# Graph convolution in three layers: more source tiles as float32r halves, count blocks loaded in fifths, and a two-input instruction on VectorE to widen the counts

## The chip, the cores and the metric

One core of a Trainium2 chip. The time is that of the device for one execution, in microseconds (us). TensorE is called PE here, VectorE DVE, ScalarE ACT, GpSimd POOL and SyncE SP, as the profile names them.

## The reference, cut to what matters

```
N, E, D, ED = 12500, 212500, 64, 16      # nodes, edges sorted by dst, row and edge widths
def conv(h, W, b):
    m = concatenate([h[dst], h[src], edge_attr], axis=1) @ W + b
    return segment_sum(m, dst, num_segments=12500)
h = relu(conv(x, W1, b1))
h = relu(conv(h, W2, b2))
out = layernorm(x + conv(h, W3, b3))
```

All in float32, with 12,500 loops (each node to itself) among the 212,500 edges.

## The kernel before, in words

Since the product is linear, the kernel sums the source rows of each target first and multiplies by `W` afterwards. The sum over edges is itself a product: a matrix of edge counts (source node by target node) times the rows. The nodes stand in 100 tiles of 125 (`TILES`), and 25 batches of 4 tiles or 500 nodes (`BATCHES`, `T`, `B`). A **batch** `g` is one group of 500 targets in one layer; `g` runs from 0 to 74, layer 0 is 0 to 24, layer 1 is 25 to 49, layer 2 is 50 to 74 (`LAST` is 50).

The first 375 targets of a batch (`DENSE`) go through the counts: for each of the 100 source tiles, a block of 125 by 375 counts in fp8. The other 125 targets (`FAR`) go edge by edge: POOL gathers their source rows with 18 indirect DMAs of 128 rows (`gather_rows`, L788), DVE makes 18 masks in one instruction (`make_far_masks`, L1182, 2250 elements a partition), and PE adds 36 small products (`sum_far`, L1519 and L1523).

Layer 0 builds the counts and stores them in HBM, then applies them. Layers 1 and 2 only load and apply them. In the program a batch of these layers is this on PE:

- Each row in float32 is kept as three bf16 parts. A source tile costs two matmuls of 375 columns: the **wide** one takes parts 0 and 1 side by side (128 columns of weights, `apply_wide`, L1461), the **narrow** one part 2 (64 columns, `apply_narrow`, L1490).
- In layer 2, 60 of the 100 tiles (the batches in `SPLIT`, 15 **units** of 4 tiles) are instead kept as two float32r halves side by side, and cost one matmul of 376 columns (`apply_split`, L1477). Its moving operand must be float32r too, so the fp8 counts of the unit's 4 tiles are first widened into a ring of 3 buffers (`spread`, `SPREAD_RING`): even units by ACT (`spread_act`, L917), odd units by DVE (`spread_dve`, L1371). A spread of unit `u` waits on `spread_used` until PE has used unit `u` - 3.
- Units and wide tiles alternate; the narrow matmuls come at the end of each of four quarters (`QUARTERS`).
- Between the quarters stand the steps of the batch before: `turn_h` (transposes) after the first, half of `conv` (the product with `W`) after the second, its other half after the third. At the end of the batch stands `sum_far`.
- After `conv`, DVE does `make_nodes` (L1255 on: in layer 1 the relu and the split into parts and halves, in layer 2 the residual and layernorm). Each engine runs its own list in order, so a spread behind `make_nodes` waits with it.

SP loads the counts in halves of 50 tiles (`load_block`), into three slots (`SLOTS`). POOL may be up to two batches ahead: `gather_rows` of batch `g` waits on `far_summed` for batch `g` - 2, and at the start of a layer for the rows of the whole layer before. The masks have two buffers and the same wait.

```
nc.vector.tensor_copy(spread[0:L, u % SPREAD_RING, :, 0:DENSE], counted(g, t, T)).then_inc(dve_spread, 1)
nc.tensor.matmul(acc_ps(g, slice(0, WIDE)), halves[0:L, i, j, :, :].rearrange("p k d -> p (k d)"),
                 spread[0:L, u % SPREAD_RING, j, :], start=(i == 0 and j == 0), stop=False)
```

Of the kernel before, what the change touches and what calls it, by code (L numbers as in the profile page):

```python
# [5 lines left out]
def gnn_kernel(nc, x, src, dst, edge_attr, weights, out):  # L6
# [18 lines left out]
    N, D = x.shape  # L25
# [30 lines left out]
    QUARTERS = [0, 24, 50, 74, TILES]  # L56
    HALF = TILES // 2
    SLOTS = 3
    WIDE = DENSE + 1
    SPREAD_RING = 3  # L60
    WHOLE = [0, 1, 4, 8, 10, 12, 15, 18, 19, 22]
    SPLIT = [b for b in range(BATCHES) if b not in WHOLE]
    UNITS_OF = [[b for b in SPLIT if QUARTERS[q] <= b * T < QUARTERS[q + 1]] for q in range(4)]
    TILES_OF = [[t for t in range(QUARTERS[q], QUARTERS[q + 1]) if t // T in WHOLE] for q in range(4)]
    assert all(b * T + T <= QUARTERS[q + 1] for q in range(4) for b in UNITS_OF[q])
# [47 lines left out]
    with ctx:  # L113
# [3 lines left out]
        def sem(name):  # L117
# [11 lines left out]
        HALVES = len(SPLIT) * T * 2 * D * 4  # L129
        halves_at = parts_at + len(SPLIT) * T * PARTS * D * 2 - HALVES  # L130
        assert halves_at % 32 == 0 and halves_at >= early_at + 4 * 768
        halves = nc.alloc_sbuf_tensor_at("halves", [P, len(SPLIT), T, 2, D], fp32r, offset=halves_at)
        staged = attr_stage[:, :, :].rearrange("p s c -> p (s c)")[:, 0:T * PARTS * D].bitcast(bf16).rearrange(
            "p (k t a d) -> p k t a d", k=2, t=T, a=PARTS)

        def whole_tile(layer, t):

            return WHOLE.index(t // T) * T + len(SPLIT) * T + t % T if layer == LAYERS - 1 else t

        blocks_at = -(-nc.sbuf_base // 32) * 32  # L140
# [63 lines left out]

        x_rows = is_key_flat[0:L, 0:4 * T * D].bitcast(fp32).rearrange(
# [101 lines left out]
        spread_used = sem("spread_used")  # L307
        spread_cleared = sem("spread_cleared")
# [20 lines left out]
        ALL = LAYERS * BATCHES  # L329
        LAST = (LAYERS - 1) * BATCHES  # L330
# [252 lines left out]
        def store_parts(engine, g):  # L583
# [36 lines left out]
        def wait_half(engine, g, t):  # L620

            n = half_of(g, t)
            engine.wait_ge(block_loaded[n % SLOTS], (n // SLOTS + 1) * DMA)

# [3 lines left out]
        def _(sp):  # L628
# [16 lines left out]
            def load_block(g, half):  # L645

                b = g % BATCHES
                n = 2 * (g - BATCHES) + half
                words = slice(half * HALF * DENSE // 2, (half + 1) * HALF * DENSE // 2)
# [64 lines left out]
            for g in range(BATCHES):  # L714
                for k in range(PER_BATCH):
# [9 lines left out]
                    if k == PER_BATCH - RING and g == BATCHES - 1:  # L725
                        for half in range(2):
                            load_block(BATCHES, half)
# [5 lines left out]
            for g in range(BATCHES + 1, ALL):  # L733
                for half in range(2):
                    load_block(g, half)
# [8 lines left out]
        def _(pool):  # L744
# [29 lines left out]
            def gather_rows(g, j):  # L774
                layer = g // BATCHES
                if j == 0:
                    if layer == 0:
                        pool.wait_ge(far_src_loaded[g % 2], (g // 2 + 1) * DMA)
                    if g % BATCHES <= 1:
                        stores = 1 if layer == 0 else BATCHES if layer < LAYERS - 1 else len(WHOLE)  # L780
                        pool.wait_ge(parts_stored[layer], stores * 2 * DMA)
                        if layer == LAYERS - 1:
                            pool.wait_ge(staged_stored[0], (len(SPLIT) + 1) // 2 * 2 * DMA)
# [893 lines left out]
```

## Time and profile before

| what | value |
| --- | --- |
| median of 3 runs | 2837.05 us (2836.85 to 2837.15) |
| the profiled execution: its own time | 2837.66 us |
| the profiled execution: its span, first to last instruction | 2835.8 us |
| PE busy | 2680.3 us, 95% of the span |
| DVE, ACT, POOL busy | 61%, 55%, 57% |
| mean granted clock of PE, as a share of full speed | 0.985 |
| moved by DMA | 498.04 MB |

Layer 0 fills the span up to 1396.7 us, layer 1 follows to about 2137 us, layer 2 to the end. The rows that the prediction reads stand further down. In a line of the timeline the columns are: start (us from the span's start), duration (us; of a run of equal instructions, the whole of it), engine, line, operation, what it writes and reads, and count; in brackets the idle time before it and what ended that. A matmul's recorded duration is longer than its share of the pipeline, so the cost of one is read from the distance between starts.

### The profile page before, as it was taken

What the parts mean: (1) busy time and instruction counts of PE and PEld (TensorE: products, weight loads), DVE (VectorE), ACT (ScalarE), POOL (GpSimd) and SP (SyncE); (2) the same over time, 40 slices, a digit from 0 to 9 for tenths busy, and PEclk for the clock granted to TensorE, in tenths of its full rate; (3) what the DMA queues carried; (4) which work ended last, traced back from release to release, by engine and by line L of the source; (5) the groups of instructions that cost most, each with busy time, mean ns of one, the idle gap of its engine ahead of it and who ended that gap; (6) DMA issues with size and microseconds to landing.
All of it is one profiled execution on the core that took longest, in us unless ns stands there. A gap on an engine that the chain in (4) does not pass through costs nothing.

```text
span 2835.8 us, 56920 instructions
## 1 busy us (share of the span) xinstructions
PE 2680.3 (95%) x21643; PEld 1690.4 (60%) x21643; DVE 1724.7 (61%) x4026; ACT 1567.2 (55%) x2535; POOL 1624.4 (57%) x1391
## 2 busy tenths in 40 slices
PE   1599999999999999999989999999998899999998
PEld 0155555555555555555656666666666666666666
DVE  7999999999999999999412111111113444444443
ACT  5699898998989989989200000000003444444444
POOL 5355344353453544535277666666644777777775
PEclk9699999999999999999999999999999999999999
DMA  4543434435344343353656666666655666666663
GB/s 94 132 137 112 176 110 144 143 110 179 108 130 159 109 168 119 113 176 110 228 195 221 207 215 214 223 218 218 220 204 185 217 227 226 241 232 223 237 239 108
DMA packets 224957, 498.04 MB, mean 176 GB/s; under 512 B 150353, under 2 KB 186183, under 8 KB 208688
## 3 DMA queue, kind: packets, MB, share of 16 engines
q1 hardware_dynamic: 120196, 277.89, 27.9%
q10 hardware_dynamic: 57404, 146.14, 13.8%
q0 software_dynamic: 47088, 70.34, 10.0%
q8 instruction: 179, 2.93, 0.4%
q14 instruction: 90, 0.74, 0.1%
HBM read 347.58 MB, written 146.61 MB: 174 GB/s over the span
## 4 chain that ended last, share of the span: by engine, by line
PE 86%; DVE 6%; POOL 3%; ACT 2%; issue 2%; DMA 1%; SPq 0%; ACTq 0%; POOLq 0%; DVEq 0%
PE ps L1461 32%; PE ps L1490 18%; PE ps L1431 14%; PE ps L1477 7%; PE ps L1558 3%; PE ps L1519 3%; PE ps L1509 3%; POOL far_rows L788 3%; PE ps L1559 2%; PE ps L1523 2%; PE ps L1544 1%; ACT spread L917 1%; PE ps L1533 1%; ACT blocks L850 1%; DVE is_key L1131 1%
## 5 line engine op out<-in xcount | busy, mean ns | idle before, releaser
L788 POOL DMA_INDIRECT far_rows<-parts,far_src x1350 | 1570.7, 1163 | 1157.1 <-DMA far_src<-in_src 570.3
L1461 PE MATMUL ps<-blocks,parts 125*128 125x375 fp8e4 x6000 | 1351.4, 325 | 4.1 <-ACT blocks L850 2.4
L850 ACT ACTIVATE blocks<-ps 128x505 fp8e4<-128x505 f32 x1875 | 1118.0, 759 | 129.3 <-PE ps L1431 126.5
L1461 PEld LDWEIGHTS ps<-blocks,parts 125*128 125x128 bf16 x6000 | 557.6, 99 | 406.4 <-issue 52.5
L1431 PE MATMUL ps<-is_key,is_low 128*128 128x505 bf16 x1875 | 701.6, 384 | 31.8 <-DMA w_own<-in_L_gnn_W 14.0
L1131 DVE TENSOR_SCALAR is_key<-from_one,parts 128x500 bf16<-128x500 f16 x1875 | 596.4, 351 | 2.0 <-PE ps L1431 1.2
L1490 PE MATMUL ps<-blocks,parts 125*64 125x375 fp8e4 x6000 | 565.8, 327 | 0.0
L1490 PEld LDWEIGHTS ps<-blocks,parts 125*64 125x64 bf16 x6000 | 309.0, 110 | 244.5 <-issue 154.0
L917 ACT CAST spread<-blocks 125x1500 fp32r<-125x1500 fp8e4 x200 | 285.9, 1442 | 266.4 <-PE ps L1477 165.6
L1477 PE MATMUL ps<-spread,halves 125*128 125x376 f32 x1500 | 365.5, 366 | 28.8 <-ACT spread L917 22.4
L1371 DVE CAST spread<-blocks 125x1500 fp32r<-125x1500 fp8e4 x175 | 167.1, 956 | 329.7 <-PE ps L1477 329.7
L1121 DVE TENSOR_TENSOR is_low<-from_one,parts 128x640 bf16<-128x640 f16 x375 | 308.2, 822 | 16.0 <-PE ps L1431 12.6
L1431 PEld LDWEIGHTS ps<-is_key,is_low 128*128 128x128 bf16 x1875 | 185.2, 100 | 216.1 <-DVE is_key L1131 31.0
L1255 DVE COPY z<-ps 125x256 f32<-125x256 f32 x51 | 21.7, 425 | 480.4 <-PE ps L1559 480.4
L1477 PEld LDWEIGHTS ps<-spread,halves 125*128 125x128 f32 x1500 | 255.4, 190 | 64.6 <-ACT spread L917 39.7
L1182 DVE SCALAR_TENSOR_TENSOR far_masks<-far_dst,from_one 128x750 fp8e4<-128x750 int32 (+1 forms) x125 | 195.0, 1560 | 156.9 <-PE ps L1523 156.9
L876 ACT ACTIVATE node_rows<-z,node_deg 125x64 f32<-125x64 f32 x200 | 54.0, 367 | 372.0 <-DVE z L1255 350.3
L923 ACT COPY acc_sb<-ps 128x500 f32<-128x500 f32 x50 | 28.9, 577 | 210.2 <-PE ps L1523 210.2
L928 ACT COPY own_sb<-ps 64x500 f32<-64x500 f32 x50 | 28.5, 570 | 192.9 <-PE ps L1544 192.9
L1166 DVE SCALAR_TENSOR_TENSOR masks<-dst_stage,from_one 128x825 bf16<-128x825 int32 x125 | 126.4, 1011 | 0.0
L1558 PE MATMUL ps<-w_src,acc_sb 128*125 128x64 f32 x600 | 124.0, 288 | 0.7 <-ACT own_sb L928 0.7
L1558 PEld LDWEIGHTS ps<-w_src,acc_sb 128*125 128x125 f32 x600 | 88.5, 186 | 47.4 <-issue 43.7
(136 smaller groups left out, 1447.7 us busy)
## 6 DMA issues: line engine op xcount, KB each, us to landing
blocks<-counts SPq DMA_DIRECT2D x100, 2343.8 KB
counts<-blocks ACTq DMA_DIRECT2D x25, 4687.5 KB, 14.6
far_rows<-parts,far_src POOLq DMA_INDIRECT x1350
attr_stage<-in_edge_attr SPq DMA_DIRECT2D x125, 88.0 KB
h_rows<-rows ACTq DMA_DIRECT2D x49, 128.0 KB
own_sb<-attr_sums ACTq DMA_DIRECT2D x49, 95.7 KB
parts<-parts SPq DMA_DIRECT2D x1, 4200.0 KB
parts<-parts SPq DMA_DIRECT2D x24, 168.0 KB
```

The costliest lines, as they stand in the source:

```text
L788: nc.gpsimd.indirect_dma_start(far_rows[:, g % 2, j, :], None, parts_d[layer], bass.IndirectOffsetOnAxis(ap=far_src[:, g % BATCHES, j:j + ...
L850: nc.scalar.activation(blocks[:, b % 2, :, n * W:(n + 1) * W], build[:, c % BUILD, 0:COLS].rearrange("p (t w) -> p t w", w=W), ACT.Copy, s ...
L917: nc.scalar.copy(spread[0:L, u % SPREAD_RING, :, 0:DENSE], counted(g, t, T)).then_inc(act_spread, 1)
L1121: nc.vector.tensor_tensor(is_low[:, m % 2, :, :], from_one[:, 0:P].rearrange("p (a l) -> p a l", a=1).to_broadcast([P, LOWS, P]), lows[:, ...
L1131: nc.vector.tensor_scalar(is_key[:, c % KEY_RING, 0:KEYS], from_one[:, :], keys[:, b, n:n + 1], None, ALU.is_equal).then_inc(keyed, 1)
L1182: nc.vector.scalar_tensor_tensor(out=far_masks[:, g % 2, js, :], in0=far_dst[:, b, js].rearrange("p (j a) -> p j a", a=1).to_broadcast(shape),
L1371: nc.vector.tensor_copy(spread[0:L, u % SPREAD_RING, :, 0:DENSE], counted(g, t, T)).then_inc(dve_spread, 1)
L1431: nc.tensor.matmul(build[:, c % BUILD, 0:COLS], is_low[:, c // LOWS % 2, c % LOWS, :], is_key[:, c % KEY_RING, 0:COLS], start=True, stop=T ...
L1461: nc.tensor.matmul(acc_ps(g), parts[0:L, layer % 2, whole_tile(layer, t), 0:2, :].rearrange("p k d -> p (k d)"), moving, start=(t == 0 and ...
L1477: last = nc.tensor.matmul(acc_ps(g, slice(0, WIDE)), halves[0:L, i, j, :, :].rearrange("p k d -> p (k d)"), spread[0:L, u % SPREAD_RING, j ...
L1490: last = nc.tensor.matmul(acc_ps(g)[side:side + D, :], parts[0:L, layer % 2, whole_tile(layer, t), 2, :], moving, start=False, stop=(t >= ...
L1558: nc.tensor.matmul(z_ps[:, t, :], acc_flat[:, at], w_src[layer][:, :], start=True, stop=False)
```

## The change: what it does

- Layer 1 from its second batch on keeps 60 tiles as halves (3 of every 5 batches, `SPLIT_OF`), layer 2 keeps 80 (4 of every 5): 15 and 20 units in a batch. The first batch of layer 1 still takes 100 whole tiles.
- A batch goes in **fifths** of 20 tiles: 3 or 4 units alternating with the wide tiles, then 8 or 4 narrow matmuls. The steps of the batch before stand after fifths 0, 1 and 2. SP loads fifths into 6 slots.
- During the first batch of layer 1, DVE adds the three bf16 parts of 60 tiles and splits the sums into halves (`halve`, 12 instructions of 256 elements a partition for each fifth, 60 in all), which lie where parts and blocks lay.
- DVE widens a unit with `scalar_tensor_tensor` (count times one, then the larger of that and count), both inputs being the same fp8 counts in SBUF.
- The order on ACT and DVE is written anew, with spreads around each of the other steps. The flags of an input that the kernel can't handle are looked at somewhat later.

```
-    QUARTERS = [0, 24, 50, 74, TILES]
-    HALF = TILES // 2
-    SLOTS = 3
+    FIFTHS = 5
+    FIFTH = TILES // FIFTHS
+    GROUP_OF = FIFTH // T
+    SLOTS = 6
...
+    SPLIT_OF = [0, 3, 4]
...
+        def units_of(g):
+
+            return SPLIT_OF[g // BATCHES] if BATCHES < g < ALL else 0
...
+                        spread_act(h, 5, 3 * m + 2)
+                    if g + 2 < ALL:
+                        load_attr(act, g + 2)
+                    spread_act(h, 3 * m + 2, 3 * m + 4)
+                    give_rows(g)
+                    spread_act(h, 3 * m + 4, FIFTHS * m)
+                    give_nodes(g)
+                spread_act(h + 1, 0, 3)
...
-                    nc.vector.tensor_copy(spread[0:L, u % SPREAD_RING, :, 0:DENSE], counted(g, t, T)).then_inc(dve_spread, 1)
+                    nc.vector.scalar_tensor_tensor(out=spread[0:L, u % SPREAD_RING, :, 0:DENSE], in0=counted(g, t, T), scalar=1.0,
+                                                   in1=counted(g, t, T), op0=ALU.mult, op1=ALU.max).then_inc(dve_spread, 1)
+
+            def halve(q):
+
+                dve.wait_ge(block_used, q + 1)
+                order = [2, 1, 0]
...
+                for r in order:
+                    step(nc.vector.tensor_tensor(sums[0:L, r, :, :], three[r][0], three[r][1], ALU.add))
...
+                nc.vector.engine_nop().then_inc(halved, 1)
...
+            for g in range(BATCHES, ALL):
+
+                h = g + 1
+                m = units_of(h)
...
+                nodes_at = 7 if h % BATCHES == 0 else 3 * m + 2
+                spread_dve(h, 3, 5)
                 if g + 2 < ALL:
                     make_far_masks(g + 2)
-                spread_dve(g + 1, [9, 11, 13] if g == LAST else [5, 7, 9, 11, 13])
...
+                spread_dve(h, 5, nodes_at)
                 make_nodes(g)
...
+                spread_dve(h, nodes_at, FIFTHS * m)
+                spread_dve(h + 1, 0, 2)
...
+                for q in range(FIFTHS):
+                    tiles = range((q * GROUP_OF + m) * T, (q + 1) * FIFTH)
+                    for i in range(m):
+                        apply_split(g, q * m + i)
+                        for t in tiles[i * len(tiles) // m:(i + 1) * len(tiles) // m]:
```

In `spread_dve(g, first, stop)` the odd units from `first` up to `stop` are meant.

**DVE in a batch of layer 2.** Before: 5 spreads (units 5 to 13), the nodes, 2 spreads (1 and 3 of the next batch), the mask, and again.

```order
L1371 CAST spread<-blocks 125x4x375 x5
L1255 COPY z<-ps 125x256
L1277 TENSOR_TENSOR z<-z,is_key 125x256
L1278 TENSOR_REDUCE mean<-z 125x4
L1279 SCALAR_TENSOR_TENSOR z<-mean,z 125x256
L1281 TENSOR_TENSOR left<-z 125x256
L1282 TENSOR_REDUCE var<-left 125x4
L1284 RECIPROCAL rstd<-std 125x4
L1286 TENSOR_TENSOR node_rows<-z,rstd 125x256
L1371 CAST spread<-blocks 125x4x375 x2
L1182 SCALAR_TENSOR_TENSOR far_masks<-far_dst,from_one 128x2250
```

In the changed kernel the same stretch, L1429 being the spread, L1311 the first line of the nodes and L1238 the mask:

```order
L1429 SCALAR_TENSOR_TENSOR spread<-blocks 125x4x375 x5
L1311 COPY z<-ps 125x256
L1333 TENSOR_TENSOR z<-z,is_key 125x256
L1334 TENSOR_REDUCE mean<-z 125x4
L1335 SCALAR_TENSOR_TENSOR z<-mean,z 125x256
L1337 TENSOR_TENSOR left<-z 125x256
L1338 TENSOR_REDUCE var<-left 125x4
L1340 RECIPROCAL rstd<-std 125x4
L1342 TENSOR_TENSOR node_rows<-z,rstd 125x256
L1429 SCALAR_TENSOR_TENSOR spread<-blocks 125x4x375 x5
L1238 SCALAR_TENSOR_TENSOR far_masks<-far_dst,from_one 128x2250
```

Behind the nodes now stand 5 spreads, of which 3 (units 15, 17 and 19) are of the batch that PE is working on, and 2 (units 1 and 3) of the next.

**PE in a batch of layer 2**, from the transposes after the first part of a batch to the first half of `conv` (L1558; L1642 after the change). Before:

```order
L1544 MATMUL ps<-ident,h_rows 64x125 x4
L1477 MATMUL ps<-spread,halves 128x376 x4
L1461 MATMUL ps<-blocks,parts 128x375 x2
L1477 MATMUL ps<-spread,halves 128x376 x4
L1461 MATMUL ps<-blocks,parts 128x375 x3
L1477 MATMUL ps<-spread,halves 128x376 x4
L1461 MATMUL ps<-blocks,parts 128x375 x2
L1477 MATMUL ps<-spread,halves 128x376 x4
L1461 MATMUL ps<-blocks,parts 128x375 x3
L1490 MATMUL ps<-blocks,parts 64x375 x10
L1558 MATMUL ps<-w_src,acc_sb 125x64
```

After the change:

```order
L1628 MATMUL ps<-ident,h_rows 64x125 x4
L1561 MATMUL ps<-spread,halves_last 128x376 x4
L1546 MATMUL ps<-blocks,parts 128x375
L1561 MATMUL ps<-spread,halves_last 128x376 x4
L1546 MATMUL ps<-blocks,parts 128x375
L1561 MATMUL ps<-spread,halves_last 128x376 x4
L1546 MATMUL ps<-blocks,parts 128x375
L1561 MATMUL ps<-spread,halves_last 128x376 x4
L1546 MATMUL ps<-blocks,parts 128x375
L1574 MATMUL ps<-blocks,parts 64x375 x4
L1642 MATMUL ps<-w_src,acc_sb 125x64
```

Between two units there is now one wide matmul in place of two or three, and 4 narrow ones close the fifth in place of 10.

## Rows read from the trace of the kernel before

**Rows 1.** Windows, one batch of each layer: length, busy (count) per engine, clock.

```profile
1613.68:1642.75 29.07, 29.07 (x260) 18.81 (x257) 5.06 (x8) 2.21 (x6) 19.17 (x18) 1.00 0.61 214
2479.34:2506.06 26.72, 25.81 (x198) 18.41 (x197) 12.15 (x18) 12.79 (x11) 21.23 (x19) 1.00 0.67 232
```

**Rows 2.** Timeline, PE, a quarter of a batch of layer 1 and `sum_far`.

```profile
1605.43 4.37 PE L1461 MATMUL ps<-blocks,parts 125*128 125x375 fp8e4 x26
1609.73 2.27 PE L1490 MATMUL ps<-blocks,parts 125*64 125x375 fp8e4 x26
1611.93 1.20 PE L1519 MATMUL ps<-far_masks,far_rows 128*128 128x125 fp8e4 x18
...
1613.68 4.05 PE L1461 MATMUL ps<-blocks,parts 125*128 125x375 fp8e4 x24
```

**Rows 3.** Timeline, PE, units in layer 2.

```profile
2491.55 0.98 PE L1477 MATMUL ps<-spread,halves 125*128 125x376 f32 x4
...
2492.57 0.98 PE L1477 MATMUL ps<-spread,halves 125*128 125x376 f32 x4
...
2493.83 0.83 PE L1490 MATMUL ps<-blocks,parts 125*64 125x375 fp8e4 x8
...
2495.48 0.94 PE L1477 MATMUL ps<-spread,halves 125*128 125x376 f32 x4
```

**Rows 4.** Waits in a stretch of layer 1 (1500 to 2000 us), POOL's own.

```profile
POOL far_rows L788 <- PE ps L1523: 73.1, 16, 4.7
```

**Rows 5.** Waits in a stretch of layer 2 (2200 to 2700 us), POOL's only entry.

```profile
POOL far_rows L788 <- issue: 103.1, 338, 0.3
```

**Rows 6.** Durations (ns, min/median/max) of the mask and of the spread on DVE.

```profile
L1182 DVE SCALAR_TENSOR_TENSOR far_masks<-far_dst,from_one x125: 924/936/2505, 136.3 to 2773.4; 128x750 fp8e4<-128x750 int32 x75, 128x2250 fp8e4<-128x2250 int32 x50
...
L1371 DVE CAST spread<-blocks x175: 933/943/1192, 2131.5 to 2814.4; 125x1500 fp32r<-125x1500 fp8e4 x175
```

**Rows 7.** Timeline, DVE and POOL, a mask in layer 1.

```profile
1425.94 0.94 POOL L788 DMA_INDIRECT far_rows<-parts,far_src  x1 [0.30 <-issue]
...
1426.43 2.48 DVE L1182 SCALAR_TENSOR_TENSOR far_masks<-far_dst,from_one 128x2250 fp8e4<-128x2250 int32 x1
1427.18 2.55 POOL L788 DMA_INDIRECT far_rows<-parts,far_src  x1 [0.30 <-issue]
```

**Rows 8.** Timeline, POOL, layer 2; 18 gathers from 2506.57 to 2533.32.

```profile
2506.57 2.96 POOL L788 DMA_INDIRECT far_rows<-parts,far_src  x1 [0.30 <-issue]
...
2512.33 1.40 POOL L788 DMA_INDIRECT far_rows<-parts,far_src  x1 [0.30 <-issue]
2514.03 1.14 POOL L788 DMA_INDIRECT far_rows<-parts,far_src  x1 [0.30 <-issue]
...
2533.32 2.96 POOL L788 DMA_INDIRECT far_rows<-parts,far_src  x1 [0.30 <-issue]
```

**Rows 9.** Timeline, DVE, layer 2: the nodes and two spreads.

```profile
2495.71 0.42 DVE L1255 COPY z<-ps 125x256 f32<-125x256 f32 x1 [1.09 <-PE ps L1559]
...
2499.00 0.43 DVE L1286 TENSOR_TENSOR node_rows<-z,rstd 125x256 f32<-125x256 f32 x1
...
2511.97 0.94 DVE L1371 CAST spread<-blocks 125x1500 fp32r<-125x1500 fp8e4 x1 [2.56 <-PE ps L1477]
2514.11 0.94 DVE L1371 CAST spread<-blocks 125x1500 fp32r<-125x1500 fp8e4 x1 [1.20 <-PE ps L1477]
```

**Rows 10.** Timeline, DVE, the nodes of one batch of layer 1.

```profile
2070.78 0.42 DVE L1255 COPY z<-ps 125x256 f32<-125x256 f32 x1 [18.41 <-PE ps L1559]
...
2073.08 0.43 DVE L1273 TENSOR_TENSOR attr_stage<-left,attr_stage 125x256 bf16<-125x256 f32 x1
```

**Rows 11.** Waits of PE from 1390 us on: for the gathered rows.

```profile
PE ps L1519 <- DMA far_rows<-parts,far_src: 18.1, 2, 9.3
```

**Rows 12.** Windows: 8 us of PE from 2150 us, after it had stood still for 3.60 us.

```profile
2150.00:2158.00 8.00, 6.80 (x20) 4.76 (x21) 2.19 (x3) 3.38 (x3) 4.25 (x5) 0.50 0.31 76
```

**Rows 13.** Timeline, PE, at that place.

```profile
2150.45 1.62 PE L1477 MATMUL ps<-spread,halves 125*128 125x376 f32 x4 [3.60 <-DVE spread L1371]
```

More of the change, by code:

```diff
@@ L55, in gnn_kernel @@
     WORDS = TILES * DENSE // 2
-    QUARTERS = [0, 24, 50, 74, TILES]
-    HALF = TILES // 2
-    SLOTS = 3
+    FIFTHS = 5
+    FIFTH = TILES // FIFTHS
+    GROUP_OF = FIFTH // T
+    SLOTS = 6
+    ALL = LAYERS * BATCHES
+    LAST = (LAYERS - 1) * BATCHES
     WIDE = DENSE + 1
     SPREAD_RING = 3
[L61 to L65, printed above, removed]
+    SPLIT_OF = [0, 3, 4]
+    assert FIFTHS * FIFTH == TILES and GROUP_OF * T == FIFTH
     J = 11
@@ L725, in _ @@
                     if k == PER_BATCH - RING and g == BATCHES - 1:
-                        for half in range(2):
-                            load_block(BATCHES, half)
+                        for q in range(FIFTHS):
+                            load_block(BATCHES, q)
                 if g >= 1:
@@ L733, in _ @@
             for g in range(BATCHES + 1, ALL):
-                for half in range(2):
-                    load_block(g, half)
+                for q in range(FIFTHS):
+                    load_block(g, q)
             for k in range(2):
@@ L903, in _, with spread_act @@
             load_attr(act, BATCHES + 1)
[L904 to L912 removed]
+            def spread_act(g, first, stop):
+                for i in range(first + first % 2, min(stop, FIFTHS * units_of(g)), 2):
+                    u = unit_at(g, i)
+                    t = batch_of(g, i) * T
+                    if i == 0 or batch_of(g, i - 2) // GROUP_OF != t // FIFTH:
+                        wait_fifth(act, g, t)
                     if u >= SPREAD_RING:
@@ L1450, in apply_wide @@
                 layer, b = divmod(g, BATCHES)
-                if t == 0 and layer < LAYERS - 1:
+                alone = t == 0 and units_of(g) == 0
+                if alone:
                     apply_start(g)
@@ L1454, in apply_wide @@
                     pe.wait_ge(parts_ready, g)
-                if layer and t % HALF == 0:
-                    wait_half(pe, g, t)
                 if layer:
@@ L1616, in _ @@
                         turn_h(g - 1)
-                    last = apply_narrow(g, tiles, max(TILES_OF[3]) - 1 if g >= LAST else TILES - 2)
-                    if q % 2:
-                        last.then_inc(block_used, 1)
+                    last = apply_narrow(g, tiles)
+                    last.then_inc(block_used, 1)
                     if g % BATCHES == 0:
```

271 lines of the change are left out of this document (151 added, 120 removed).

## Prediction

> **What bounds the kernel now.** The change leaves layer 0 alone, so I read layers 1 and 2. First the windows of one batch of each: in layer 1 PE is busy for all of its 29.07 us, at full clock, and in layer 2 for 25.81 of 26.72 us [rows 1]. Layer 1 is bound by PE. In layer 2 a second engine stands at its limit, which a table of shares hides: POOL. Its waits tell it. In the 500 us shown of layer 1, POOL waits in 16 of 17 batches for `sum_far`, by up to 4.7 us [rows 4]; in layer 2 its only idle time is the pause of 0.3 us between two gathers [rows 5]. It does exactly 18 gathers in the 26.75 us between two rows of [rows 8], the length of a batch.
>
> A gather that nothing disturbs takes 0.94 us, and the next starts 0.30 us later [rows 7]: 1.25 us for each, 22.5 us for a batch. The rest comes from DVE. In [rows 7] the mask runs from 1426.43 to 1428.91; the gather that starts inside it, at 1427.18, ends at 1429.73, 0.82 us behind the mask's end, while the one that had started 0.49 us before the mask took its plain 0.94 us. So a gather has something to do in its first tenth of a microsecond that can't be done while such a two-input instruction runs, and after that it is not disturbed. A spread by CAST disturbs both ends: the gather at 2512.33 starts inside one and takes 1.40 us, the one at 2514.03 starts 0.08 us before one and takes 1.14, until just behind its end [rows 8, 9].
>
> **What the matmuls give.** From distances between starts in [rows 2]: a wide matmul is 4.30 / 26 = 0.165 us, a narrow one 2.20 / 26 = 0.085, so a whole tile is 0.25. All that is not tiles in a batch of layer 1 is 29.07 - 25.0 = 4.07 us. In [rows 3] a unit with two wide matmuls takes 1.02 us, so a split matmul is (1.02 - 0.33) / 4 = 0.172, and a unit followed by narrow ones 1.26: 0.24 us more for the change of shape, which comes four times now and five times then. A split tile saves 0.078 us.
> - Layer 1: 60 x 0.172 + 40 x 0.25 + 5 x 0.2 + 4.07 = 25.4 us of PE in 24 batches, 3.7 less than 29.07.
> - Layer 2: 80 x 0.172 + 20 x 0.25 + 1.0 + 4.07 = 23.8 us in 25 batches, 2.9 less than 26.72.
>
> If nothing else counted, 24 x 3.7 + 25 x 2.9 = 161 us would go.
>
> **What the new spread costs DVE.** A mask of 750 elements takes 0.93 us, one of 2250 takes 2.50 [rows 6]: 1.05 ns for each element more, so 1500 elements in this form take 0.93 + 0.79 = 1.72 us, against 0.94 by CAST. With a wait on each side I reckon 1.75. The bounds are 0.94 (if it keeps the speed of the CAST) and 2.50 (the whole mask).
>
> **Where PE then waits for DVE.** I lay a batch of layer 2 out from t = 0, the end of the second half of `conv` (behind unit 11). A unit is 4 x 0.172 + 0.165 = 0.85 us; a fifth 3.4 + 0.2 + 0.34 = 3.95. In [rows 3, 9] it is at 2495.48, where the next unit starts on PE, and DVE's nodes run from 2495.71 to 2499.43; with the next start DVE is 3.95 us behind t = 0. The spread of unit 15 stands behind them (it stood before no unit of the same batch before), so it ends at 5.7; PE has done units 12 to 14 at 2.55 and waits 3.2 us. Unit 17 and 19 follow closely; PE is through with the batch, `sum_far` (1.75 us, [rows 2]) included, at 12.9. Unit 3 of the next batch waits for unit 0 to be used and ends at 15.4, the mask at 17.9, unit 5 at 19.65; PE would need it at 18.1: 1.6 us more. After that DVE keeps up, and the next t = 0 comes at 28.6 us. In layer 1 the same: nodes 2.73 us [rows 10], unit 11 ready at 4.7 where PE has come to 2.2, so 2.5 us of waiting and 28.0 us for a batch. ACT's spreads are ready in time everywhere, so they cost nothing; if they were late, the worst is the 0.8 to 1 us per batch that they cost now (in the 0.9 us idle of [rows 1]).
>
> **What the new spread costs POOL.** Both inputs of it lie in SBUF, as with the mask, so I take it that a gather's start waits for its end. Where spreads run back to back, POOL then starts one gather per 1.75 us instead of one per 1.25. Counting in the layout above, start by start (the first at the end of the instruction that blocked, the next 1.12 us behind it, then every 1.25 us, unless DVE is inside a spread or a mask again), gives 16 gathers in the 28.6 us of layer 2 and 16 in the 28.0 us of layer 1. 18 are needed. The missing two come while PE stands before `sum_far` and DVE has nothing to spread: at most 2.5 us more, at least 1.45, since the last one must only start there. Layer 2: 30.5 us (30.1 to 31.1). Layer 1: 29.6 us (29.5 to 30.5). Below, the bound is no blocking at all; above, each spread finds the gathers at random, and costs its length less half of 1.25 and less 0.13 (1.25 - 1.12), that is 0.97 us; the mask costs 1.7 by the same rule, and 7 or 10 spreads over 24.2 us give 31.0 and 33.9 us. I take the count, since start follows on start in the same order in every batch, as the equal rows of a batch apart show [rows 8].
>
> The Trainium skill speaks against this step (SBUF — State Buffer, "Who interferes with whom"): two SBUF inputs on DVE contend only with a GpSimd instruction that reads SBUF, and it infers that generating descriptors needs only the write interface, which would leave the gathers alone and make the sum the one of rival A. The trace agrees with the first half and not with what follows from the second: the gather behind the mask did wait [rows 7].
>
> **The start of layer 1.** POOL's first 36 gathers of a layer decide when PE can end its second batch; PE waited for them twice, 18.1 us together [rows 11]. They now meet seven spreads (7 x 0.8) and the 60 small instructions of `halve` (0.43 us at most each, about 20 gathers beside them, 0.2 us apiece): 9 us later, bounds 3 and 18. `halve` itself lasts about 12 x 0.4 = 4.8 us for a fifth that PE needs 20 x 0.25 = 5 us for, and is hidden behind it; if it were not, each of five fifths could be late by a microsecond. The start of layer 2 is in that layer's 25 x 30.5. The 250 smaller loads for 100 carry the same bytes, five fifths ahead of their use; I cost them at nothing, bound 1 us per batch.
>
> **Sum.** Layer 1: 23 x (29.6 - 29.07) + 9 = +21. Layer 2: 25 x (30.5 - 26.72) = +94.5. Together +115 on the profiled execution's 2837.7 us, which stands 0.6 us above the median: 2953 us.
>
> **The rivals.**
> - **A, the spread does not block POOL.** Then 22.5 + 1.7 = 24.2 us of POOL is under the chain, which gives 28.0 and 28.6: 24 x (-1.07) + 25 x 1.9 = +22, or 2860 us. For it: the spread is fp8 and reads the same address twice, and no row shows such an instruction. Against: the masks in [rows 7, 8].
> - **B, faster: PE hardly waits for DVE.** POOL free as in A, and the gaps before units 15 and 5 (11 in layer 1) filled, because a unit is used later than I laid out or the spread is as short as a CAST. PE binds at 25.4, POOL and PE at 24.4: 24 x (-3.7) + 25 x (-2.3) = -146, or 2692 us. It decides where PE's waiting falls below 3.3 us a batch, 161 / 49; with half of my gaps it gives about 2776. For it: in layer 2 now, PE waits under 1 us a batch on spreads [rows 1]. Against: the order, which puts 4 us of nodes before unit 15, with two units in hand.
> - **C, the clock falls too.** After 3.60 us without work PE ran 8 us at half of full clock [rows 12, 13]. If each gap of 3 us brings that, 8 us of work take 4 more per batch of layer 2, of which the gap before `sum_far` takes up 1.9: +2 x 25 to +4 x 25, or 3000 to 3050 us.
>
> **How the numbers follow.** My forecast 0.5, A 0.2, B 0.18, C 0.12. The time is that of the first, 2953. The range is 2790 to 3040: it holds the forecast with the count's bounds (29.5 and 30.1 with 3 us at the start: 2935; 30.5 and 31.1 with 18: 3000), A, most of C and the slow edge of B, and leaves out the rest of B and C and the random case of 33.9, together under 0.2. About 0.2% (6 us) can be told from no change here. Faster is B and the part of A whose gaps are shorter than laid out: 0.19. Same 0.04. Slower 0.77.
>
> **What would show it.** Spreads on DVE near 1.72 us. Gathers of 2 us and more, each ending 0.82 us behind a spread. PE waiting for DVE's spread before unit 15 in every batch, about 3 us, and for gathered rows before `sum_far` in most batches of layer 2. Batches of 29.6 and 30.5 us. I am wrong if gathers beside spreads take 0.94 us (A), or if PE's waits for spreads are under 1 us (B).

## The result and the profile after

The changed kernel takes 2914.95 us (median of 4 runs, 2913.84 to 2917.39), the kernel before 2836.95 us beside it (2836.69 to 2837.15). The ratio is 1.0276, 95% interval 1.0258 to 1.0294: slower, as forecast, by 78 us where 115 were laid out, and inside the range. The profiled execution took 2914.92 us with a span of 2913.1, 77.3 us more than that of before.

Where the 77.3 us lie can be read from the starts of the second half of `sum_far` on PE (L1607, before L1523), one group of rows in each batch, so that two neighbours are one batch apart (us; sums can miss by 0.1 through rounding):

| stretch | before | after | difference | forecast |
| --- | --- | --- | --- | --- |
| to the end of layer 0 | 1395.3 | 1394.3 | -1.0 | 0 |
| layer 1, first two batches | 70.7 | 71.8 | +1.1 | +9 |
| layer 1, the other 23 | 670.4 (29.15 each) | 652.9 (28.39 each) | -17.5 | +12 |
| layer 2, first two batches | 72.7 | 74.9 | +2.2 | |
| layer 2, the other 23 | 615.3 (26.75 each) | 708.0 (30.78 each) | +92.7 | |
| layer 2, both together | | | +94.9 | +94.5 |

So layer 2 lost what it was forecast to lose, and layer 1 gained a little where it was forecast to lose a little. Whether the steps to these numbers hold is another question, and the answer differs.

Windows of single batches, two of layer 1 and one of layer 2, in the columns of [rows 1]:

```profile
1580.00:1609.50 29.50, 27.37 (x198) 19.18 (x196) 16.63 (x15) 13.66 (x14) 23.71 (x20) 0.94 0.66 214
1637.50:1665.48 27.98, 25.85 (x198) 18.34 (x196) 16.66 (x15) 13.66 (x14) 22.50 (x19) 1.00 0.69 224
2596.30:2627.00 30.70, 27.10 (x179) 19.61 (x178) 22.41 (x19) 15.67 (x13) 24.90 (x19) 0.94 0.63 203
```

PE was busy for all of 29.07 us in layer 1 before; now 2.13 us of the batches shown are idle. In layer 2 it idles for 3.60 us where it idled for 0.91. And the clock, 1.00 in both rows of before, is 0.94 in nearly all batches of layer 2 and in every third or fourth of layer 1: those are the batches of 29.5 us, the others take 27.3 to 28.0. The two batches of layer 1 shown idle for the same 2.13 us, so their difference of 1.52 us is the time of the same matmuls, in part at the lower clock.

The groups of POOL's gathers and of DVE's spread, as the profile's page has them (count, then busy us, mean ns, and the idle time before):

```profile
L837 POOL DMA_INDIRECT far_rows<-parts,far_src x1350 | 1743.2, 1291 | 1050.6 <-DMA far_src<-in_src 572.8
...
L1429 DVE SCALAR_TENSOR_TENSOR spread<-blocks 125x1500 fp32r<-125x1500 fp8e4 x418 | 711.8, 1719 | 397.9 <-PE ps L1561 394.9
```

The spread costs 1.72 us, to the hundredth what the masks' slope had given. PE's waits from 1390 us on (for what, us in total, times, longest), to be held against [rows 11]:

```profile
PE ps L1561 <- DVE spread L1429: 131.8, 71, 5.1
...
PE ps L1603 <- DMA far_rows<-parts,far_src: 27.8, 6, 9.3
```

PE waits for DVE's spread, as laid out. But it waited for gathered rows only 6 times in 50 batches, where the forecast had "most batches of layer 2". Of the 71 waits for a spread, 34 lie in 17 batches of layer 2 (58.6 us, 3.4 us a batch), two in each.

### The profile page after: what moved, and what is told of

Its sections match the earlier page's. It is cut to its first block, busy times and chain, and to the rows that moved or that the text cites. A ratio compares the mean times of both kernels' runs of the same rounds, so it can differ in the third digit from the quotient of the medians.

```text
span 2913.1 us, 54250 instructions
## 1 busy us (share of the span) xinstructions
PE 2641.5 (91%) x19703; PEld 1715.9 (59%) x19703; DVE 2282.0 (78%) x4339; ACT 1913.1 (66%) x2777; POOL 1795.1 (62%) x1391
## 4 chain that ended last, share of the span: by engine, by line
PE 74%; DVE 11%; POOL 8%; issue 4%; ACT 1%; DMA 1%; SPq 0%; ACTq 0%; POOLq 0%; DVEq 0%
PE ps L1546 20%; PE ps L1561 15%; PE ps L1517 13%; PE ps L1574 12%; POOL far_rows L837 7%; DVE spread L1429 4%; PE ps L1642 3%; PE ps L1603 3%; PE ps L1593 3%; PE ps L1643 2%; PE ps L1607 1%; PE ps L1628 1%; PE ps L1617 1%; ACT blocks L899 1%; DVE is_key L1187 1%
## 5 line engine op out<-in xcount | busy, mean ns | idle before, releaser
L837 POOL DMA_INDIRECT far_rows<-parts,far_src x1350 | 1743.2, 1291 | 1050.6 <-DMA far_src<-in_src 572.8
L1546 PE MATMUL ps<-blocks,parts 125*128 125x375 fp8e4 x4060 | 1113.0, 328 | 3.9 <-ACT blocks L899 2.2
L1429 DVE SCALAR_TENSOR_TENSOR spread<-blocks 125x1500 fp32r<-125x1500 fp8e4 x418 | 711.8, 1719 | 397.9 <-PE ps L1561 394.9
L964 ACT CAST spread<-blocks 125x1500 fp32r<-125x1500 fp8e4 x442 | 637.4, 1443 | 580.0 <-PE ps L1561 513.5
L1546 PEld LDWEIGHTS ps<-blocks,parts 125*128 125x128 bf16 x4060 | 370.9, 99 | 340.2 <-issue 87.1
L1561 PE MATMUL ps<-spread,halves_last 125*128 125x376 f32 x2000 | 479.0, 378 | 84.8 <-DVE spread L1429 80.3
L1561 PEld LDWEIGHTS ps<-spread,halves_last 125*128 125x128 f32 x2000 | 355.2, 201 | 129.2 <-DVE spread L1429 101.1
L1574 PE MATMUL ps<-blocks,parts 125*64 125x375 fp8e4 x4060 | 431.0, 335 | 0.0
L1517 PEld LDWEIGHTS ps<-is_key,is_low 128*128 128x128 bf16 x1875 | 185.4, 100 | 215.5 <-DVE is_key L1187 28.3
L1561 PE MATMUL ps<-spread,halves_kept 125*128 125x376 f32 x960 | 236.8, 369 | 5.1 <-DVE spread L1429 5.1
L1238 DVE SCALAR_TENSOR_TENSOR far_masks<-far_dst,from_one 128x750 fp8e4<-128x750 int32 (+1 forms) x125 | 194.8, 1559 | 13.5 <-PE ps L1607 13.5
L1561 PEld LDWEIGHTS ps<-spread,halves_kept 125*128 125x128 f32 x960 | 165.7, 195 | 24.7 <-issue 6.7
L1642 PE MATMUL ps<-w_src,acc_sb 128*125 128x64 f32 x600 | 124.0, 289 | 0.9 <-ACT own_sb L975 0.9
```

What stands on the lines that cost most here:

```text
L837: nc.gpsimd.indirect_dma_start(far_rows[:, g % 2, j, :], None, parts_d[layer], bass.IndirectOffsetOnAxis(ap=far_src[:, g % BATCHES, j:j + ...
L964: nc.scalar.copy(spread[0:L, u % SPREAD_RING, :, 0:DENSE], counted(g, t, T)).then_inc(act_spread, 1)
L1238: nc.vector.scalar_tensor_tensor(out=far_masks[:, g % 2, js, :], in0=far_dst[:, b, js].rearrange("p (j a) -> p j a", a=1).to_broadcast(shape),
L1429: nc.vector.scalar_tensor_tensor(out=spread[0:L, u % SPREAD_RING, :, 0:DENSE], in0=counted(g, t, T), scalar=1.0, in1=counted(g, t, T), op0 ...
L1517: nc.tensor.matmul(build[:, c % BUILD, 0:COLS], is_low[:, c // LOWS % 2, c % LOWS, :], is_key[:, c % KEY_RING, 0:COLS], start=True, stop=T ...
L1546: nc.tensor.matmul(acc_ps(g), parts[0:L, layer % 2, whole_tile(layer, t), 0:2, :].rearrange("p k d -> p (k d)"), moving, start=alone, stop ...
```

## The gap and what follows it

DVE in a batch of layer 2 (timeline, the columns as before), to be held against [rows 9]: two spreads, the nodes from 2613.18 to 2616.88, then the spreads of units 15 and 17, then those of units 1 and 3 after an idle time of 2.41 us.

```profile
2608.78 3.52 DVE L1429 SCALAR_TENSOR_TENSOR spread<-blocks 125x1500 fp32r<-125x1500 fp8e4 x2 [1.43 <-PE ps L1561]
2613.18 0.42 DVE L1311 COPY z<-ps 125x256 f32<-125x256 f32 x1 [0.88 <-PE ps L1643]
...
2616.46 0.42 DVE L1342 TENSOR_TENSOR node_rows<-z,rstd 125x256 f32<-125x256 f32 x1
2616.81 3.35 DVE L1429 SCALAR_TENSOR_TENSOR spread<-blocks 125x1500 fp32r<-125x1500 fp8e4 x2
2622.57 3.51 DVE L1429 SCALAR_TENSOR_TENSOR spread<-blocks 125x1500 fp32r<-125x1500 fp8e4 x2 [2.41 <-PE ps L1561]
```

PE at that place (timeline): the fifth of units 8 to 11 from its first start to the first half of `conv` behind it, then unit 14, a gap, unit 15, unit 16.

```profile
2607.81 0.93 PE L1561 MATMUL ps<-spread,halves_last 125*128 125x376 f32 x4
...
2612.05 0.43 PE L1642 MATMUL ps<-w_src,acc_sb 128*125 128x64 f32 x2
...
2615.05 0.95 PE L1561 MATMUL ps<-spread,halves_last 125*128 125x376 f32 x4
2615.84 0.34 PE L1546 MATMUL ps<-blocks,parts 125*128 125x375 fp8e4 x1
2618.58 1.33 PE L1561 MATMUL ps<-spread,halves_last 125*128 125x376 f32 x4 [2.40 <-DVE spread L1429]
...
2620.95 1.58 PE L1561 MATMUL ps<-spread,halves_last 125*128 125x376 f32 x4
```

With t = 0 at 2612.95, the end of `conv`, unit 15 starts at 5.63; the prediction had 5.7. The distance from unit 14 to unit 15 is 3.53 us, of which one unit is 0.85. What the sum left out shows in the durations behind the gap: 1.33 and 1.58 us for a unit that takes 0.95 ahead of it. Windows before, in and behind this place:

```profile
2612.95:2618.50 5.55, 3.09 (x17) 2.15 (x16) 4.75 (x10) 3.07 (x3) 4.33 (x5) 1.00 0.71 226
2618.50:2622.40 3.90, 3.82 (x14) 2.33 (x15) 1.65 (x2) 1.44 (x1) 3.11 (x3) 0.56 0.37 68
2622.40:2627.60 5.20, 5.20 (x58) 3.92 (x57) 3.44 (x2) 2.89 (x2) 4.17 (x4) 1.00 0.80 254
```

The granted clock is 0.56 in the 3.90 us behind the gap, so nearly all of that stretch ran at the lower level, and 1.00 on both sides. Unit 15 to unit 17 took 3.83 us (2618.58 to 2622.41); at full clock the layout gives two units and 4 narrow matmuls with the change of shape, 2 x 0.85 + 0.34 + 0.2 = 2.24 us. That is 1.6 us, and the next spreads of DVE, which wait until these units are used, start later by it (the 2.41 us of idle DVE above).

Whether a whole batch is longer by that can be seen in one batch of layer 2 in which the clock did not fall, beside the next one, in which it did. The first has the same two waits for a spread, of 1.06 and 2.41 us:

```profile
2351.07:2380.28 29.21, 25.61 (x177) 18.82 (x177) 22.20 (x19) 14.75 (x13) 24.03 (x18) 1.00 0.62 201
2380.28:2410.96 30.68, 27.07 (x179) 19.74 (x177) 22.39 (x20) 15.67 (x14) 24.89 (x20) 0.94 0.65 208
```

So the lower clock costs 1.5 us of a batch, and without it a batch takes 29.2 us, 0.6 more than the 28.6 laid out. That rest is no wait for POOL either: a fifth takes 4.24 us (2607.81 to 2612.05) where 3.95 were laid out, and the second gap is shorter than laid out, 1.06 us for 1.6.

## POOL behind the spread

POOL beside the two spreads that run from 2608.78 to 2612.30 and the two from 2616.81 to 2620.16 (timeline, to be held against [rows 7, 8]):

```profile
2608.47 0.94 POOL L837 DMA_INDIRECT far_rows<-parts,far_src  x1 [0.30 <-issue]
2609.71 1.60 POOL L837 DMA_INDIRECT far_rows<-parts,far_src  x1 [0.30 <-issue]
2611.62 1.49 POOL L837 DMA_INDIRECT far_rows<-parts,far_src  x1 [0.30 <-issue]
...
2617.35 1.99 POOL L837 DMA_INDIRECT far_rows<-parts,far_src  x1 [0.30 <-issue]
2619.64 1.33 POOL L837 DMA_INDIRECT far_rows<-parts,far_src  x1 [0.30 <-issue]
```

The block is there: the gather of 2611.62 ends at 2613.11, 0.81 us behind the spread's end, that of 2619.64 at 2620.97, 0.81 us behind the other pair's end, and those of 2609.71 and 2617.35 end 0.8 to 0.9 us behind the middle of the pair, where the first spread gives way to the second. The gather of 2608.47, begun 0.31 us ahead of a spread, took its plain 0.94. The mean of all gathers rose from 1163 to 1291 ns. How many fit into a batch is read over 17 batches of each layer (windows; POOL's count is the fifth in brackets), with PE's waits for rows in those of layer 2:

```profile
1552.70:2033.52 480.82, 447.16 (x3335) 315.45 (x3334) 280.63 (x247) 232.23 (x238) 387.25 (x308) 0.98 0.68 222
2288.24:2811.00 522.76, 458.90 (x2995) 333.51 (x2993) 381.15 (x323) 266.45 (x221) 425.54 (x320) 0.95 0.64 203
```

```profile
PE ps L1603 <- DMA far_rows<-parts,far_src: 2.6, 2, 1.7
```

In layer 2 POOL did 18.8 gathers a batch where PE uses 18, so it gained on PE. At the plain 1.25 us these would take 23.5 us of the 30.75; the other 7.2 us are the block, by the spreads and the mask. By an estimate from these two numbers a batch of 28.6 us has room for (28.6 - 7.2) / 1.25 = 17.1 gathers, and not 16, and 18 need 29.7 us. In layer 1, with 18.1 gathers and 5.6 us of block in 28.3 us, 17.9 fit into 28.0 us, and 18 need 28.1. POOL was the runner-up in layer 2 and level with the chain in layer 1, not the pace.

## The experiments

The theory after the result, T1: DVE's order (the nodes ahead of unit 11 or 15) makes a gap on PE, the clock falls behind it, and that is the whole of a batch; POOL's block costs only at the starts of layers. The rival, T2: POOL's block is what binds, and the gap fills time in which PE would wait for rows anyway. Four kernels ran once each, and the kernel before took 2835.93 us beside them. The four runs of the changed kernel lie within 3.6 us, so the differences of 12 us and more below stand clear of that. Batches are counted as in the table above.

### One: the spread as a CAST again

```
-nc.vector.scalar_tensor_tensor(out=spread[...], in0=counted(g, t, T), scalar=1.0, in1=counted(g, t, T), op0=ALU.mult, op1=ALU.max)
+nc.vector.tensor_copy(spread[...], counted(g, t, T))
```

> The changed kernel (2915 us) with one part undone: DVE widens by CAST again. Theory 1 (the time is set by DVE's own list: 4 us of nodes, then the spread that PE waits for, and by the clock that falls after gaps over 3 us): the waits before unit 15 and unit 5 shrink by 0.78 us each, the gap before unit 15 falls to 2.75 us and the clock holds, so layer 2 goes from 30.7 to 27.6 us a batch and layer 1 from 28.2 to 27.2: about 2815 us. Theory 2 (POOL's gathers set it, blocked by the spreads): a CAST costs the gathers 0.4 us in place of 0.6 or more, so that layer 2 goes to 22.5 + 1.7 + 10 x 0.4 = 28.2 us with PE waiting for gathered rows in most batches: about 2835 us.

Measured: 2802.39 us, 1.2% under the kernel before and below the figures of both theories. Layer 1 takes 27.26 us a batch, layer 2 27.32. PE and POOL waits over 17 batches of layer 2, and the windows of 17 batches of layer 1, of 17 of layer 2, and of two single ones of layer 2:

```profile
POOL far_rows L837 <- issue: 94.2, 309, 0.3
...
PE ps L1560 <- DVE spread L1429: 27.2, 17, 1.6
```

```profile
1547.94:2010.41 462.47, 439.56 (x3334) 311.73 (x3332) 189.33 (x247) 232.22 (x238) 369.18 (x307) 1.00 0.72 230
2243.67:2708.04 464.37, 429.82 (x2995) 321.36 (x2994) 257.57 (x323) 264.77 (x221) 370.47 (x309) 0.99 0.71 227
...
2296.63:2325.15 28.52, 26.50 (x179) 19.63 (x177) 14.98 (x19) 15.58 (x14) 22.73 (x20) 0.94 0.71 226
2325.15:2352.23 27.08, 25.04 (x179) 18.76 (x177) 15.18 (x19) 15.58 (x14) 21.59 (x19) 1.00 0.70 223
```

With the short spread the longer gap is 1.6 us and the second one is gone. The clock stays up in layer 1 and in most of layer 2, but not in all: in 3 of these 17 batches it is 0.94, and they take 28.5 us where the others take 27.1. POOL never waits for anything but its own pause: 1.51 and 1.50 us for each gather, times 18 is 27.1 and 27.0, level with the batch. But PE waits for a spread in 17 of 17 batches of each layer, for gathered rows in 3 of those of layer 1 (2.0 us together) and in none of layer 2. So DVE's order still sets the pace, and POOL stands right behind it. The two-input instruction by itself costs 2914.95 - 2802.39 = 113 us: 80 in the 23 batches of layer 2 (30.78 against 27.32), 26 in those of layer 1 (28.39 against 27.26), 7 at the starts of the layers.

### Two: the same 1.72 us with one input

```
+spread_sum = sb("spread_sum", [L, 4])
+n = spreads_to(g, i)
+if n > 4:
+    dve.wait_ge(dve_spread, n - 4)
+nc.vector.tensor_scalar(spread[...], counted(g, t, T), 1.0, 0.0, ALU.mult, ALU.add, accum_out=spread_sum[:, n % 4:n % 4 + 1])
```

> The changed kernel with DVE's spread as a tensor_scalar (count times one, plus zero) that also writes the sum of each partition to a scratch word: one SBUF input, and I expect the same 1.72 us. Theory 1: the length on DVE is the same, so the time stays at 2915 us within 10, while the gathers beside spreads fall back to 0.94 us. Theory 2: without the block the time falls to about 2860 us. If the accumulating form is shorter (about 0.94 us), it is e1 without any block: 2815 us.

Measured: 2896.19 us. DVE's time is the same and the block is gone (timeline, DVE and POOL, layer 2):

```profile
2608.66 1.72 DVE L1433 TENSOR_SCALAR_CACHE_REDUCE spread<-blocks 125x1500 fp32r<-125x1500 fp8e4 x1 [2.50 <-PE ps L1565]
2609.27 0.94 POOL L838 DMA_INDIRECT far_rows<-parts,far_src  x1 [0.31 <-issue]
2610.30 0.09 DVE L1433 DVE_READ_ACCUMULATOR spread<-blocks 125x1 f32 x1
2610.30 2.50 DVE L1239 SCALAR_TENSOR_TENSOR far_masks<-far_dst,from_one 128x2250 fp8e4<-128x2250 int32 x1
2610.52 3.10 POOL L838 DMA_INDIRECT far_rows<-parts,far_src  x1 [0.30 <-issue]
```

The gather that starts inside the spread takes 0.94 us; the next starts inside the mask, which still has two inputs, and ends 0.82 us behind it, at 2613.62. The Trainium skill (SBUF — State Buffer, "Who interferes with whom") leaves the form of `tensor_scalar` that also writes out its accumulator out of the operations that can take the ports shared with GpSimd, and here the trace agrees. Its inference that descriptors need the write interface, which would leave the gathers alone beside two inputs, does not foretell what these gathers did. A gather here also takes its row numbers from SBUF (`far_src`), and whether that read is what waits, no run tells.

Waits over 17 batches of layer 2:

```profile
POOL far_rows L838 <- PE ps L1611: 105.7, 17, 6.4
...
PE ps L1565 <- DVE spread L1433: 58.7, 34, 2.4
```

POOL now waits 6.2 us a batch, and the batch is what it was: 28.33 us in layer 1 (28.39), 30.68 in layer 2 (30.78). Taking the spread's block away gave nothing in the steady batches (layer 2 of experiment three, where it is unchanged, came out at 30.67). Of the 18.8 us by which this kernel is faster, 16.7 lie in the first two batches of each layer, 66.5 for 71.8 and 63.5 for 74.9, where PE waits for 36 gathers made in one go. T1 holds for the kernel as changed.

### Three: the nodes one unit later, in layer 1

The nodes then stand behind the spread of unit 11; DVE has one spread more done when it turns to them.

```
-nodes_at = 7 if h % BATCHES == 0 else 3 * m + 2
+nodes_at = 7 if h % BATCHES == 0 else 3 * m + 3 if m == 3 else 3 * m + 2
```

> The changed kernel with one place moved: in layer 1 the nodes stand behind the spread of unit 11 in place of before it (layer 2 as it is). Theory 1: the wait of 2.1 to 2.5 us before unit 11 goes, unit 13 is ready at 4.75 us where PE needs it at 5.3, and a batch of layer 1 takes 25.6 to 26 us: 24 x (-2.4) = -55, about 2860 us. Theory 2: POOL, which did 18 gathers in 28 us with nothing to spare, holds layer 1 at 27.5 to 28 us, PE waits for gathered rows instead: 2900 to 2915 us.

Measured: 2927.79 us, 13 more than the changed kernel and more than either theory had. Window and wait of 17 batches of layer 1:

```profile
1555.81:2044.40 488.59, 447.94 (x3333) 322.44 (x3332) 282.75 (x247) 232.30 (x238) 395.92 (x305) 0.97 0.67 218
```

```profile
PE ps L1603 <- DMA far_rows<-parts,far_src: 40.6, 17, 5.1
```

The wait for the spread is gone to the last, and in its place stands one for gathered rows, in 17 of 17 batches. A batch takes 29.03 us, between 26.9 and 32.0, where 18 gathers at 488.59 / 305 = 1.60 us need 28.8. So T2 is right about this kernel: right behind the gap stands POOL's block, and the one had been hidden by the other.

### Four: 60 split tiles in layer 2 too

```
-SPLIT_OF = [0, 3, 4]
+SPLIT_OF = [0, 3, 3]
```

> The changed kernel with 60 tiles as halves in layer 2 too (15 units in place of 20), so layer 2 has PE's order of layer 1. By PE's work alone layer 2 costs 20 x 0.078 = 1.6 us a batch more: 2954 us. Theory 1: DVE has 7 spreads in place of 10, only the gap before unit 11 is left (nodes 3.95 us, so 3.5 us of gap and the clock falls): 29 to 30 us a batch in place of 30.7: 2875 to 2900 us. Theory 2: POOL, with 3 blocks fewer, falls to 28.5 us a batch: 2860 us.

Measured: 2902.11 us, layer 2 at 30.49 us a batch for 30.78, though a quarter of the units is gone (and 20 tiles more are whole, 1.6 us of PE by the layout). Wait and window of 17 batches of layer 2:

```profile
PE ps L1561 <- DVE spread L1429: 54.0, 17, 3.2
```

```profile
2280.18:2798.48 518.30, 464.20 (x3335) 322.74 (x3334) 293.96 (x272) 220.90 (x187) 377.38 (x315) 0.95 0.64 204
```

One gap of 3.2 us before unit 11 (the nodes of layer 2 are longer than those of layer 1, and layer 1's gap is 2.1), and the clock at 0.95 again. PE idles for 3.18 us a batch where it idled for 3.76. With 15 units the second gap is gone, but the chain keeps its main two parts, the nodes and the slow matmuls behind them.

### All three edits together

If the gap and the block hide one another, single edits can't show what they cost. So one kernel takes all three: one input, 60 tiles, the nodes later in both layers. A second one has the CAST in place of the one-input form, to tell whether the block or DVE's time is left.

> Three edits to the changed kernel together: DVE's spread with one SBUF input (as in e2_one_input), 60 tiles as halves in layer 2 too (as in e4_sixty), and in both layers the nodes behind the spread of unit 11 (as in e3_nodes_later). If DVE's order and POOL's blocks are the two bounds, one behind the other, neither is left: layer 1 at 25.5 us a batch (was 29.1 before the change), layer 2 at 26.0 (was 26.7), and the layers' starts 5 and 10 us shorter: about 2730 us, 4% faster than the kernel before. If something else is next (ACT, the loads of the counts, whose rate rises by 14%), layer 1 stays at 27 us or more: 2760 us or above.

> As b1_one_input_later, but DVE spreads by CAST (0.94 us, blocks both ends of a gather). If POOL is then the bound, PE waits for gathered rows in most batches and both layers stand near 22.5 + 1.7 + 7 x 0.4 = 27.0 us a batch: about 2790 us, with the gathers at 1.19 us in the mean. If the block does not count, the shorter spread makes it as fast as b1 or faster: 2725 us.

Measured: 3640.35 us and 3202.15 us, where the kernel before took 3572.4 beside them, a quarter more than its 2837. The same two kernels again:

> The kernel of b1_one_input_later once more: on the chip of that run the kernel before took 3572 us in place of 2837, layer 0 included, so nothing can be read from it. Expected as there: about 2730 us, layer 1 at 25.5 us a batch and layer 2 at 26.0, if DVE's order and POOL's blocks are the two bounds; 2760 us or above if a third one (ACT, the loads) stands close behind.

> The kernel of b2_cast_later once more, for the same reason. POOL as the bound: both layers near 27.0 us a batch with PE waiting for gathered rows, about 2790 us. Block without weight: 2725 us.

Measured: 3651.81 and 3246.01 us, the kernel before 3584.23. Once more, with the kernel of experiment one beside them:

> The kernel of b1 again, since b1 and b3 ran beside a kernel before that itself needed 3572 and 3584 us. If the time of the changed kernel comes only from the late nodes (with the clock after the gap) and from POOL's block, nothing of either is left here: about 2730 us, 25.5 us a batch in layer 1 and 26.0 in layer 2, PE's waits for the DVE spread below 10 us over 17 batches. If a third bound is near (DVE's own busy time, or POOL's 18 gathers of 1.3 to 1.5 us each), 2760 us or more, with PE waiting for gathered rows in every batch.

> The kernel of b2 again, for the same reason. The CAST is as long as the mask's (0.94 us where the one-input form takes 1.72), but gathers wait for it. If POOL's block is what is left, about 2790 us, PE waits for gathered rows in most batches, 27.0 us a batch in both layers, and the one-input form wins by 60 us. If DVE's busy time were the next bound, it would be the CAST that wins, with 2700 to 2730 us.

> The kernel of e1 again, timed in rounds beside the two others: 2802 us, 1.2 per cent under the kernel before, if the first time holds. Against b6, whose nodes come later and whose layer 1 splits 60 tiles as this one's does, it tells what the late nodes cost where the spread is short: nothing if POOL paces (27.3 us a batch in both), 20 us or more if DVE's order does.

Measured: 3639.97, 3214.73 and 3187.71 us, the kernel before 3567.57. In these three sets all kernels ran long, the kernel before by 26%. The same stretch of 130 us (1700 to 1830) of the kernel of experiment one, PE's waits here:

```profile
PE ps L1573 <- issue: 15.8, 8, 3.7
PE ps L1560 <- issue: 12.1, 4, 5.4
```

and in its first run:

```profile
PE ps L1560 <- DVE spread L1429: 6.3, 5, 1.5
PE ps L1602 <- DMA far_rows<-parts,far_src: 0.8, 1, 0.8
```

PE stands for up to 5.4 us between instructions that wait for nothing the profile shows. What held it is not in the trace, and nothing is concluded from these times. It was not the device by itself: one of them gave 2835.93 us for the kernel before at first and 3567.57 later, another 3572.4 and then 2837.75, beside the last run. That was the kernel with all three edits once more:

> The kernel of b1 once more, alone: one-input spread, 60 split tiles in layers 1 and 2, nodes one unit later where m is 3. If the late nodes with the clock behind the gap, and POOL's block, are all that the change costs, about 2730 us (25.5 us a batch in layer 1, 26.0 in layer 2) where the kernel before takes 2836. If a third bound is near, 2760 us or more. Where the kernel before takes some 3570 us again, only the ratio can be read: 1.02 as in b1, b3 and b5.

Measured: **2727.24 us** (median of 4, 2725.14 to 2727.75) where the kernel before took 2837.75 (2836.50 to 2838.36): ratio 0.9611, 95% interval 0.9595 to 0.9627. It is 188 us under the changed kernel. Windows of 17 batches of layer 1 and layer 2, and of one batch of each:

```profile
1539.12:1974.02 434.90, 434.90 (x3334) 312.12 (x3333) 280.47 (x360) 232.00 (x238) 334.66 (x317) 1.00 0.76 246
2193.83:2633.51 439.68, 439.12 (x3335) 310.90 (x3333) 295.74 (x391) 218.91 (x187) 336.36 (x316) 1.00 0.75 241
...
1600.00:1625.58 25.58, 25.58 (x199) 18.36 (x197) 16.76 (x22) 13.65 (x15) 19.79 (x20) 1.00 0.76 246
2500.00:2525.86 25.86, 25.82 (x197) 18.27 (x197) 17.39 (x23) 12.88 (x11) 19.38 (x19) 1.00 0.76 240
```

POOL's and PE's waits in those 17 batches of layer 2:

```profile
POOL far_rows L838 <- PE ps L1611: 9.1, 7, 1.3
...
PE ps L1565 <- DVE spread L1433: 0.2, 1, 0.2
```

PE is never idle in layer 1 and for 0.56 us of 440 in layer 2, at full clock. The batches take 25.6 and 25.9 us, where "What the matmuls give" had 25.4 for a batch with 60 split tiles of layer 1: with PE left to bind, the term for 60 tiles is right to 0.2 and 0.5 us. The sum of the prediction put 0.2 for each change of shape where its own rows give 0.24; with these it gives 25.6. POOL waits for PE by at most 1.3 us; it is the next bound, with 1.06 + 0.30 us a gather, 24.5 us for 18.

The three edits alone gave -18.8, +12.8 and -12.8 us, in sum -18.8; together they give -188. The sum is not quite a fair one, since alone the later nodes stood in layer 1 only; in layer 2 they were run with the other edits alone. In layer 1, where each edit was also run by itself, the comparison is clean: a batch took 28.39 us, 28.33 with one input, 29.03 with the later nodes, and 25.62 with both. That is what two bounds in a row look like: the one behind keeps what the one in front lets go.

## Why the prediction was right or wrong

- **The spread's cost, 1.72 us: right** (1.719 mean over 418).
- **Where PE waits for DVE: right.** Unit 15 at 5.63 us for 5.7; in layer 1 a gap of 2.13 us for 2.5, and 27.3 to 28.0 us for the batches at full clock where 28.0 were laid out. The second gap, 1.6 us before unit 5, was 1.06 in the batch shown.
- **The block of POOL: right as a mechanism.** It was the step that the inference of the Trainium skill (SBUF — State Buffer, "Who interferes with whom") spoke against, and the gathers end 0.81 us behind the spreads. Rival A therefore falls, though its batch of 28.0 us, with POOL off the pace, is nearly what layer 1 did (28.39).
- **"16 gathers in the 28.6 us of layer 2 and 16 in the 28.0 us of layer 1": wrong, the step that failed.** By what the trace shows, 17 and 17.9 fit. The count laid spreads back to back and began each gather at the worst place of one; in the trace DVE idles 2.4 us between pairs, and where a gather falls shifts from pair to pair. In layer 1 the count made 29.6 us out of 28.0 and so +12 out of -25. Measured: -17.5, the chain's 28.0 and 0.4 us of clock (1.5 us in 6 of the 23 batches).
- **Layer 2, +94.5 forecast and +94.9 measured: the sum right, its last part for the wrong reason, so that the match is luck.** The 2.1 us from 28.6 to 30.7 are not POOL's 1.9. About 1.5 are rival C: the clock falls behind the gap of 2.4 us (3.5 from start to start). The other 0.6 lie in PE's fifths, 4.24 us for 3.95. Rival C was given 0.12 and an addition on top of POOL's; it came in place of it. Experiment two settles that: POOL free, and still 30.68 us. The half-clock row stood among the rows of before [rows 12, 13], and a layout that puts a gap of 3.2 us in each batch should have priced its aftermath in the main sum.
- **The start of layer 1, +9: wrong, +1.** POOL's 36 gathers took 52.8 us from the first start for 47.9 before, so +4.9 for the forecast's 9.6, and began 1.6 us earlier. PE's one wait for rows there fell from 9.3 to 6.3 us, and a wait of 5.1 us for a spread came to it. That the block does cost at the starts shows in experiment two, which got 5.3 us back there, and 11.4 at the start of layer 2.
- **Rival B, PE hardly waits: wrong for this kernel, and the last experiment is what it described.** With the nodes moved by one unit, one input on the spread and 60 tiles in layer 2, PE's waiting fell to nothing, and the time, 2727 us, is 35 above what B gave for 80 tiles.

What stays open: whether the later nodes would serve 80 split tiles as well as 60 wasn't tried; PE was busy for 25.0 us in a batch of 80 at full clock (experiment one) and for 25.8 in one of 60 (the last), so there is less than 1 us a batch in it. Whether the CAST with the later nodes beats the one-input form on an undisturbed chip isn't known either; by the 1.50 us a gather of experiment one POOL would bind it near 27 us a batch. And the later nodes in layer 2 with the two-input spread left in place were not run, so how the 112 us by which its 23 batches fell (30.78 to 25.91 us each) divide among the three edits is not known.

## What to carry to other kernels

When two resources are within a microsecond of each other, an edit that frees one shows nothing or even a loss, so try the edits together before dropping them: in a batch of layer 1 here, one edit alone gave -0.1 us, the other +0.6, and both together -2.8. Look for a long vector step that stands in the list ahead of a short one that the matrix engine needs soon; moving it by one unit took the gap away, and the gain came once the next bound was moved too. And price an idle gap on PE with the slow matmuls that may follow it, 1.5 us here for gaps of 2 to 3 us, not by its own length alone.

## What the runs showed of the hardware

- Two forms of one widening, both 1.72 us for 1500 elements, differ in what they do to GpSimd: beside the one with two inputs a gather took up to 1.99 us in the batch shown, beside the accumulating one with one input 0.94. The CAST, 0.94 us, slows gathers too. Over 17 batches of layer 2 the mean gather took 1.33 us with the two-input form, 1.20 with the CAST and 1.06 with the one-input form, where the masks alone are left to slow it.
- PE stood idle for 2.40 us before unit 15 of layer 2, and the 3.90 us behind it ran at a mean of 0.56 of the full clock, in nearly every batch; in one batch with the same gap the clock stayed at 1.00. The gap of layer 1, 2.13 us, was followed by a batch at 0.94 in every third or fourth case. With 1.6 us, in experiment one, the clock fell in 3 of 17 batches of layer 2. Such a batch is 1.5 us longer.
- The same kernels, some minutes apart, took 2802 and 3188 us, and 3640 and 2727 us, with the kernel before moving between 2836 and 3584 beside them. The ratios moved too, 1.02 for the kernel that is 0.961 undisturbed, so a ratio is only worth something where the yardstick stands where it stood.
